# A one-core vision layer on TensorE: the first images' grey computed on DVE, the key projection as three fp32r products, and the experts' output added to the stored residual by DMA transfers

## The reference

```python
gray  = einsum('bchw,c->bhw', x, (0.2989, 0.587, 0.114))
edge  = (|conv3x3(gray, scharr_x)| + |conv3x3(gray, scharr_y)|) / 2      # h
n     = layernorm(h);  ns = n shifted by one token
k, v, r = (n*tm_i + ns*(1-tm_i)) @ W_i.T        for i in k, v, r
y     = wkv(w, u, k, v)                          # running max, two scans over the tokens
h     = h + (sigmoid(r) * y) @ Wo.T
n2    = layernorm(h);  e = argmax(n2 @ Wg.T)    # one of 8 experts per token
h     = h + gelu((layernorm(n2)*s_e + b_e) @ W1_e + b1_e) @ W2_e + b2_e  # result
```

## Time and profile before

| what | value |
|---|---|
| median of the runs | 1195.4 us |
| the profiled execution | 1192.23 us |
| its span, first to last instruction | 1190.7 us |
| PE busy, share | 1109.3 us, 93% |
| DVE busy, share | 1003.7 us, 84% |
| ACT busy, share | 858.2 us, 72% |
| mean granted TensorE clock | 0.981 of full |

### The profile page before, as it was taken

One profiled execution on the slowest core, in us unless ns is written; L12 is line 12 of the kernel. 1 busy time (PEld: TensorE's weight loads), 2 busy tenths in 40 slices (PEclk: granted clock), 3 DMA queues, 4 the chain that ended last, 5 costly groups with the idle time before them and its releaser, 6 DMA issues.

```text
span 1190.7 us, 16854 instructions
## 1 busy us (share of the span) xinstructions
PE 1109.3 (93%) x5571; PEld 696.7 (59%) x5571; DVE 1003.7 (84%) x1828; ACT 858.2 (72%) x1380; POOL 177.3 (15%) x242
## 2 busy tenths in 40 slices
PE   1277799999999999999999999999999999999997
PEld 0033366666666666656666666656666666666666
DVE  1257999999998999999999999999998999999971
ACT  2046788777777787777777877777778877777652
POOL 5211101111111110111110101111101111110000
PEclk9967899999999999999999999999999999999999
DMA  7997756776676766776767667766766677662001
GB/s 187 207 169 121 133 127 128 149 154 140 136 151 150 139 134 134 158 143 135 147 146 146 132 129 159 153 132 136 158 145 123 137 149 153 141 102 47 18 18 36
DMA packets 164837, 157.79 MB, mean 133 GB/s; under 512 B 12528, under 2 KB 164678, under 8 KB 164678
## 3 DMA queue, kind: packets, MB, share of 16 engines
q1 hardware_dynamic: 129990, 123.84, 42.7%
q0 software_dynamic: 34816, 33.56, 22.3%
HBM read 105.96 MB, written 68.17 MB: 146 GB/s over the span
## 4 chain that ended last, share of the span: by engine, by line
PE 90%; DMA 3%; DVE 3%; ACT 2%; SPq 1%; issue 0%; POOL 0%; POOLq 0%; DVEq 0%
PE bank L1008 28%; PE bank L1144 18%; PE bank L1074 15%; PE bank L1002 10%; PE bank L1050 9%; PE bank L1096 4%; DMA rows_in<-gray_dram 2%; PE bank L1122 2%; PE bank L1145 1%; DMA gray_dram<-planes 1%; PE bank L1087 1%; PE bank L1131 1%; PE bank L1063 1%; SPq L329 1%; DMA scharr_dj<-in_L_tok_scharr_dram 0%
## 5 line engine op out<-in xcount | busy, mean ns | idle before, releaser
L1144 PE MATMUL bank<-w_sb,hidden 128*128 128x256 f32 x1024 | 238.8, 380 | 0.8 <-ACT hidden L860 0.8
L1144 PEld LDWEIGHTS bank<-w_sb,hidden 128*128 128x128 f32 x1024 | 184.6, 190 | 29.2 <-ACT hidden L860 1.5
L1002 PE MATMUL bank<-rows_in,conv_w 102*32 102x512 f32 x1024 | 129.9, 628 | 31.5 <-DMA rows_in<-gray_dram 31.5
L1008 PE MATMUL bank<-mixed_k,w_k_t 128*128 128x512 f32 x256 | 127.5, 622 | 4.1 <-DVE mixed_k L557 4.1
L1008 PE MATMUL bank<-mixed_r,w_r_t 128*128 128x512 f32 x256 | 118.6, 607 | 4.8 <-DVE mixed_r L557 4.8
L1074 PE MATMUL bank<-normed_hi,w_hi 128*128 128x512 f32 x256 | 122.2, 477 | 0.0
L1008 PE MATMUL bank<-mixed_v,w_v_t 128*128 128x512 f32 x256 | 120.1, 592 | 0.0
L568 DVE TENSOR_TENSOR_SCAN max_state<-neg_exp_w,bank 128x256 f32<-128x256 f32 x128 | 80.7, 672 | 45.3 <-PE bank L1008 45.3
L1050 PE MATMUL bank<-w_o_t,rwkv 128*128 128x256 f32 x512 | 117.5, 382 | 0.0
L403 POOL TENSOR_TENSOR pool_turn<-pool_turn 128x1 f32<-128x1 f32 x32 | 7.9, 246 | 663.1 <-ACT planes L784 663.1
L1050 PEld LDWEIGHTS bank<-w_o_t,rwkv 128*128 128x128 f32 x512 | 94.9, 190 | 12.0 <-issue 0.5
(11 more groups left out here) (132 smaller groups left out, 2230.5 us busy)
## 6 DMA issues: line engine op xcount, KB each, us to landing
rows_in<-gray_dram SPq DMA_DIRECT2D x192, 256.0 KB
planes<-in_x_dram SPq DMA_DIRECT2D x128, 256.0 KB, 5.0
gray_dram<-planes POOLq DMA_DIRECT2D x128, 256.0 KB, 6.1
gray_dram<-in_x_dram SPq DMA_DIRECT2D x64, 256.0 KB, 6.5
out_dram<-resid SPq DMA_DIRECT2D x64, 256.0 KB, 2.2
rows_in<-gray_dram SPq DMA_DIRECT2D x128, 24.0 KB
gray_dram<-rows_in SPq DMA_DIRECT2D x1, 1032.0 KB
hidden<-in_L_ffn_W_dram SPq DMA_DIRECT2D x2, 256.0 KB, 10.3
```

The lines of the kernel that those rows point to most:

```text
L1002: ins = pe.matmul(bank[BANK_EDGE[n]][ROW_TILE * q:ROW_TILE * (q + 1), :], conv_w[0:TAPS, c, :], rows, start=True, stop=True)
L1008: ins = pe.matmul(ps[:, :], w_t[i][:, kt, ct * P:(ct + 1) * P], mixed[i][:, 2 * kt:2 * kt + 2, :].rearrange("p i t -> p (i t)"), start=(kt ...
L1144: pe.matmul(ps, hidden[:, m, i, rows], w2_sb[:, m, :], start=(m == 0), stop=False)
```

## The change

Five things are changed together.

1. The grey of pairs 0 and 1 is computed on DVE from planes loaded by SP and ACT (`first_gray_of`), and stored to `gray_dram` in one go. From pair 2 on (`has_later`) the way of the grey is as before.
2. `rows_in` has two buffers. SP's step loads the planes and the blue earlier than before, behind other waits.
3. The key projection takes three fp32r products per half, of `w_hi`, `w_lo`, `part_hi`, `part_lo`. ACT makes the high part of the mixed input (`high_part`), DVE the low part (`low_part`).
4. DVE's `result` is gone. SP stores the residual already in the PROJ stage. ACT copies the experts' output from PSUM to `y_out` (`copy_y`), and POOL starts two transfers that add it to the stored output (`add_y`).
5. The orders of all engines, the PSUM banks and the places of the setup are new. `route_logits` and `copy_logits` moved from the end of a step to the start of the next.

```diff
+FIRST = 2
+SPLIT = (0,)
+    def has_later(self, stage):
+        return self.has(stage) and (not isinstance(self.j, int) or UNROLL * self.j + self.u - stage >= FIRST)
-        rows_in = sb("rows_in", [P, TILES, 2, D])
+        rows_in = [sb(f"rows_in{i}", [P, TILES, 2, D]) for i in range(2)]
+        y_out = [sb(f"y_out{i}", [P, NB, D]) for i in range(2)]
...
@@ SP step
+                if at.has_later(LOAD):
+                    b = at.buf(LOAD)
+                    wait(sp, s_green, at.count(LOAD, 16 * HALF, 16 * HALF, back=2 + FIRST))
...
+                    load_plane(0, at.j, at.u, b)
+                    wait(sp, s_edge_ps, at.count(LOAD, 4, 4, back=3))
+                    load_plane(1, at.j, at.u, b)
+                    wait(sp, rows_loaded[b], at.dma_count(LOAD, X_DMAS, back=2))
+                    load_blue(at.j, at.u, b)
+                if at.has_later(GRAY):
...
+                    for i in range(2):
+                        load_rows(sp, b, i)
+                if at.has(PROJ):
+                    b = at.buf(PROJ)
                     for half in range(HALF):
+                        wait(sp, s_resid, at.count(PROJ, 2, half + 1))
+                        sp.dma_start(out_rows(at.j, at.u - PROJ, half), resid[b][:, 2 * half:2 * half + 2, :]
+                                     ).then_inc(stored[b], 16)
@@ POOL
+            def add_y(at):
+                if not at.has(FFN):
+                    return
+                b = at.buf(FFN)
+                wait(pool, s_out_turn, at.count(FFN, 1, 0))
+                wait(pool, stored[b], at.dma_count(FFN, HALF))
+                wait(pool, s_y_out, at.count(FFN, 2, 2))
+                pool.tensor_tensor(out_turn[:, :], out_turn[:, :], out_turn[:, :], ALU.add).then_inc(s_out_turn, 1)
+                for half in range(HALF):
+                    pool.dma_start(out_rows(at.j, at.u - FFN, half), y_out[b][:, 2 * half:2 * half + 2, :],
+                                   accum_op=ALU.add).then_inc(added[b], 16)
@@ DVE
+            def first_gray_of(i):
+                for half in range(HALF):
+                    rows = slice(2 * half, 2 * half + 2)
+                    total = first_gray[i][:, rows, 1:D + 1]
+                    dve.wait_ge(first_in[i][half], 48)
+                    dve.scalar_tensor_tensor(out=total, in0=planes[i][:, rows, 0, :],
+                                             scalar=GRAY_WEIGHTS[0] / GRAY_WEIGHTS[2], in1=first_blue[i][:, rows, :],
+                                             op0=ALU.mult, op1=ALU.add).then_inc(s_first_mix, 1)
...
+            def low_part(i, stage, low_done, at):
...
+                dve.tensor_tensor(part_lo[i][:, :, :], mixed[i][:, :, :], part_hi[i][:, :, :].bitcast(F32),
+                                  ALU.subtract).then_inc(low_done, 1)
-            def result(half, at):
...
@@ PE
+                products = [(w_t[i], mixed[i])]
+                if i in SPLIT:
+                    products = [(w_hi[i], part_hi[i]), (w_lo[i], part_hi[i]), (w_hi[i], part_lo[i])]
...
@@ ACT
+            def high_part(i, stage, high_done, at):
...
+                act.activation(part_hi[i][:, :, :], mixed[i][:, :, :], ACT.Copy).then_inc(high_done, 1)
+            def copy_y(half, at):
...
+                act.activation(y_out[b][:, 2 * half:2 * half + 2, :], pair_view(bank[BANK_Y[half]]), ACT.Copy
+                               ).then_inc(s_y_out, 1)
             def step(at):
-                scaled(0, at)
-                scaled(1, at)
                 absolute(0, at)
+                copy_logits(at)
                 reciprocal(at)
                 absolute(1, at)
                 absolute(2, at)
+                scaled(0, at)
+                scaled(1, at)
                 absolute(3, at)
```

More of the change, by code:

```diff
@@ L311, in step @@
             def step(at):
-                if at.has(LOAD) and not at.first():
-                    wait(sp, s_green, at.count(LOAD, 16 * HALF, 16 * HALF, back=2))
-                    load_planes(at.j, at.u, at.buf(LOAD))
-                if at.has(LOAD) or at.has(GRAY):
-                    wait(sp, s_edge_ps, at.count(LOAD, 4, 4, back=2))
-                if at.first():
-                    sp.wait_ge(s_borders, 32)
-                if at.has(LOAD):
-                    load_blue(at.j, at.u, at.buf(LOAD))
@@ L660, in best_logit @@
             def best_logit(at):
-                if not at.has(PROJ):
+                if not at.has(FFN):
                     return
-                wait(dve, s_logits, at.count(PROJ, 1, 1))
+                wait(dve, s_logits, at.count(FFN, 1, 1))
                 dve.tensor_reduce(best[:, :], logits, AXIS_X, ALU.max).then_inc(s_best, 1)
@@ new lines, in _, with decay_rate @@
+            act.wait_ge(s_cleared, CLEARED_B2)
+            for r, src in rows:
+                act.dma_start(params_raw[r:r + src.shape[0], :], src).then_inc(s_params_in, 16)
+            act.dma_start(w_raw[2], Wr.rearrange("(a p) c -> p a c", p=P)).then_inc(s_w_in, 16)
+            act.wait_ge(first_stored[1], 16 * HALF)
+            load_rows(act, 1, 1)
+            def decay_rate(at):
+                if not at.is_step(EDGE):
+                    return
+                act.wait_ge(s_dve_setup, SETUP_PARAMS)
+                act.activation(exp_w[:, :], params[:, ROW_W:ROW_W + CH], ACT.Exp).then_inc(s_act_setup, 1)
@@ L1016, in project_k @@
                 if ct == 0:
-                    wait(pe, s_mix_k, at.count(WKV, 1, 1))
-                else:
-                    wait(pe, s_normed2_lo, at.count(WKV, 2, 1, back=2))
+                    wait(pe, s_low_k, at.count(WKV, 1, 1))
+                elif ct == 1:
+                    wait(pe, s_abs, at.count(WKV, 4, 1, back=-1))
                 project(0, ct, bank[BANK_K[ct]], s_k_ps)
@@ L1045, in output_projection @@
                 if half == 0:
-                    wait(pe, s_abs, at.count(PROJ, 4, 4, back=-2))
                     wait(pe, s_rwkv, at.count(PROJ, 1, 1))
+                elif half == 1:
+                    wait(pe, s_abs, at.count(PROJ, 4, 2, back=-2))
                 for i in range(2):
@@ L1057, in transpose_route @@
                     return
-                wait(pe, s_abs, at.count(FFN, 4, 2, back=-3))
                 wait(pe, s_route, at.count(FFN, 1, 1))
@@ L1102, in transpose_normed2 @@
                 if ct == 0:
-                    wait(pe, s_hidden, at.count(PROJ, 4, 1, back=1))
                     wait(pe, s_normed2, at.count(PROJ, 1, 1))
@@ L1137, in second_layer @@
                     wait(pe, s_hidden, at.count(FFN, 4, 4))
-                else:
-                    wait(pe, s_gate, at.count(FFN, 2, 1, back=-2))
                 for i in range(2):
```

532 lines of the change are left out of this document (310 added, 222 removed).

## The result

The changed kernel takes 1179.98 us (median of 4 runs, 1178.11 to 1180.79), the kernel before 1194.87 beside it. The ratio is 0.9873, with a 95% interval of 0.9854 to 0.9892: 1.3% faster. The profiled execution has a span of 1177.8 us, against 1190.7.

The account below looks back on a forecast made before the run. PE was taken to set the steady step, with the grey's loop closing it after the change. Filling -18, steady part +2 and emptying +6 sum to -10, on 1195.4 giving 1185 us, range 1166 to 1222.

Parts of the forecast that it names:

- The likeliest case: Steady steps: the grey closes the step at 33.4 to 34.4 us, giving 1172 to 1200 us; chance 0.50.
- The loop: Way of the grey, once per step: red's turn 8.0, red 7.5, green 6.7, rows 11.5; with jitter, 33.9 us.
- The steady term: The 27 steady steps: 33.9 us each, 0.1 more than before, together +2 us.
- Red's open length: Red's accumulating transfer in the loop: between 6.9 and 9.75 us, taken as 7.5.
- The rival of 1242 us: Steady steps: red stays at 9.75 us, the grey bounds a step of 36.0 us, +47 us; chance 0.27.
- The adding transfer: `add_y` on POOL: issued 1 to 2 us into the step, its traffic ending at about 8 to 9.
- PE's work: Key products on PE: two halves save 0.68 us a step, so PE needs 33.1 us.
- The filling: Start of the program up to pair 4's convolution, which comes at 153: -18 us (10 to 24).
- The emptying: End of the program: last copy and accumulating transfer +4, `low_part` wait in step 34 +2.8 less 0.7; together +6 us.
- The clock rival: Steady steps: waits at step starts drop PE to 1.2 GHz, loop 37.1 us, +77, 1272 us; chance 0.05.

Follow-up runs that it names:

- e1: The changed kernel with the two scalings of the planes back at the head of ACT's step from step 5 on; 1164.8 us (ratio 0.9763).
- e2: The changed kernel with the key projection again as f32 products, without high_part and low_part; 1186.38 us (ratio 0.9937).
- e11: The changed kernel with red and green planes from pair 2 on loading 16 of 256 columns, scaling set to 0.5; 1164.73 us (ratio 0.9764).
- e5: The kernel before with the two scalings behind the third absolute value of the edges from step 5 on; 1193.95 us (ratio 1.0005).
- e4: The changed kernel with the adding transfer moving only 16 of the 256 columns of each row; 1179.92 us (ratio 0.9883).
- e6: The kernel before with only the key projection changed to three fp32r products (high_part on ACT, low_part on DVE); 1180.09 us (ratio 0.9894).
- e3: The changed kernel with scalings early from step 5 on and the key projection again in f32; 1179.6 us (ratio 0.9876).
- e7: The changed kernel with all pairs' grey by accumulating DMA, the first two too, and the padded buffer zeroed whole; 1207.94 us (ratio 1.0129).
- e9: As e7, against the changed kernel, but with the scalings at the head of every step of ACT; 1182.44 us (ratio 0.9916).
- e10: The changed kernel with scalings at the head of every step and the later weights one step later in SP's queue; 1160.23 us (ratio 0.9725).

## Why the prediction was right

Forecast 1185, range 1166 to 1222; measured 1180.0. The likeliest case, the grey closing the step at about its old length, is what happened. The sum was -10 and became -12.9 in the profiled spans (14.9 in the medians), but two terms were off by 7 and 8 us, in opposite directions. That they nearly cancel is luck.

- **The loop.** Right in mechanism, shown by e1 and e2: the idle time stands before `convolve(0)`, its releaser is "DMA rows_in", and the split's gain mostly vanishes into it. I had 8.0 + 7.5 + 6.7 + 11.5 and a little for jitter, 33.9; the means are 7.56 + 6.98 + 6.84 + 12.22 = 33.60. Turn and red were too long by 0.4 and 0.5, and the rows 0.7 too short, so that the four added up to 33.7 by luck too. On the rows, the read of the earlier trace rows is of a quiet moment, while now the DMA share at the same point is 1.1. I had the next planes move in the first 8 to 9 us of a step; they are issued 6.4 us ahead of `convolve(0)` (624.75, 631.17), while the rows are still on their way, and e11 shows what that costs. The window:

```profile
629.00:630.00 1.00, 1.00 (x7) 0.74 (x5) 1.00 (x3) 1.00 (x2) 0.00 (x0) 1.00 1.09 221
```

- **The steady term, +2, measured -5.9.** The mis-sized term: 33.9 against 33.60, 0.3 us a step times 27 is 8 us. Of the 0.3, 0.2 are what I added for jitter. Every guess of a tenth in a loop that runs 27 times weighs 3 us.
- **Red's open length.** I set 7.5 between 6.9 and 9.75, arguing that it starts when the traffic is nearly over. e5 shows the later start as cause: moved alone, it drops from 9.71 to 7.13. That it is the traffic of the planes fits their landings, but no run removed them beside an early red. The rival of 1242 us needed 9.75 in the late place, and there was none.
- **The adding transfer.** I took its traffic as ended by 8 to 9 us; it lands at 9.0, and by e4 its last 1.5 us beside the red cost nothing. In e1, where the red starts 1.5 us behind it, the red takes 8.9 in the mean. The Trainium skill, DMA: Bandwidth & Descriptors, section Queues, rings and completion order, says that each DMA engine takes the descriptors of a queue in order. In e1 the trace agrees: the adding transfer lands at 9.3 us, the two halves of the red at 11.6 and 13.4. That this order is what makes e1's red longer is not shown, since before, with no adding transfer, the red took 9.71 us at that place.
- **PE's work.** 0.68 predicted for the split, 0.64 (before to e6) and 0.65 (e3 to e1) measured. PE needs 32.9 a step, not 33.1. The other 0.3 are in e3 too (33.53 against 33.82, both without waits), so they come with the rest of the change, in which the products stand in another order. I had not priced that, and haven't taken it apart.
- **The filling, -18, measured -11.3.** The first convolution came at 33.3, not 28, pair 1's at 48.4, not 43, pair 2's at 86.65, not 84: its scaling ended at 58.9, not 57, its red's turn came at 59.66, and the 27 us from there were as predicted. Pairs 2 to 4 were to take 34.5 us each, and took 34.69 and 37.94. In the second PE waits for `low_part`, and its clock falls for a while. PE's timeline:

```profile
128.85 0.57 PE L1167 MATMUL bank<-part_k_hi,w_k_hi 128*128 128x512 f32 x1 [2.59 <-DVE part_k_lo L651]
```

The windows around it (the clock is the third number from the end):

```profile
126.00:131.00 5.00, 2.41 (x10) 1.70 (x7) 5.00 (x6) 5.00 (x8) 0.00 (x0) 0.81 0.00 0
131.00:136.00 5.00, 5.00 (x21) 4.10 (x20) 3.80 (x8) 0.97 (x2) 2.59 (x3) 0.84 0.53 54
```

I had found that wait for step 34 and not asked for it here, the other step where DVE's list runs behind. Without the split (e2, e3) this step takes 36.3 us. But e1 keeps the split and takes 35.8, without that wait and at a mean clock of 0.92, so how much of the 37.94 is the split's stays open. And I missed what e7 showed: late scalings cost the filling too, 16.5 us when all pairs go the old way. With them the early grey is worth 34 us (e7 to the changed kernel), and much of it pays for the late scalings; with early ones it is 19.6 (e9 to e10, which also differ in the place of the later weights).
- **The emptying, +6, measured +4.4.** PE waits 2.54 us at step 34's key products, as worked out (2.8), and the last transfer ends 7.85 us after the turn. Before, the last addition started 3.5 us ahead of the end: +4.35, where I had 4. The other 2.1 us (2.8 less 0.7) did not appear: from pair 31's `convolve(0)` to that last turn or addition it is 103.4 us in both kernels, so some 2 us came back elsewhere, and I haven't taken that apart. The two lines:

```profile
1102.60 0.50 PE L1167 MATMUL bank<-part_k_hi,w_k_hi 128*128 128x512 f32 x1 [2.54 <-DVE part_k_lo L651]
...
1169.95 0.18 POOL L469 TENSOR_TENSOR out_turn<-out_turn 128x1 f32<-128x1 f32 x1 [13.64 <-ACT y_out L1031]
```

The size also depends on the execution. The emptying of e5 runs the same operations as before's, yet takes 2.9 us longer, at a granted clock of 0.97 instead of 1.00 (before, then e5):

```profile
1083.82:1190.70 106.88, 97.14 (x492) 67.24 (x484) 69.40 (x133) 55.56 (x90) 0.00 (x0) 1.00 0.07 23
1084.63:1194.40 109.77, 99.99 (x492) 69.08 (x484) 69.46 (x133) 55.58 (x90) 0.00 (x0) 0.97 0.07 22
```

- **The clock rival.** It did not come for good: over the 907 us the granted clock is 1.00 in the mean. But it showed once. Behind the longest wait at a step's start, 1.89 us, PE fell to its 1.2 GHz level, and the convolution took 4.38 us instead of 2.78. PE's timeline, and the windows behind it:

```profile
732.27 4.38 PE L1157 MATMUL bank<-rows_in,conv_w 102*32 102x512 f32 x24 [1.89 <-DMA rows_in<-gray_dram]
...
733.00:734.00 1.00, 1.00 (x12) 0.28 (x8) 1.00 (x2) 0.60 (x1) 1.00 (x2) 0.65 0.59 156
734.00:736.00 2.00, 2.00 (x16) 0.49 (x12) 0.76 (x2) 0.00 (x1) 1.84 (x2) 0.50 1.04 255
736.00:737.00 1.00, 1.00 (x20) 0.59 (x16) 0.00 (x0) 0.00 (x0) 0.00 (x0) 0.64 0.93 171
```

In e4 the same happened behind a wait of 1.93 us at 329.3, and not behind those of 1.84 and 1.79. So this kernel was closer to the clock rival than its mean clock says.

So the steady part gains 23.8 us with early scalings (27 x 0.88, e1), of which the split gives 17.3 (e6), and the late scalings take 17.8 of it back (27 x 0.66). The early grey's gain is partly a repair of what late scalings do to the filling. The additions by DMA were not needed for the step and cost 4.35 us at the end. Undoing the late scalings alone is worth 15.2 us by the medians and 13 by the ratios, about as much as the whole change (14.9).

## What to carry to other kernels

Write out every loop that must close once per step, with its slack, and compare its length with the bounding engine's work; an edit that makes that engine cheaper is worth only as much as the loops have slack. When an operation moves, recompute the transfer behind it at its new time: traffic that it met before may be gone. And an order that only delays something in steady state may tie steps together in the filling, where there is no steady overlap to hide it.

## What the runs showed of the hardware that was not expected

- The same accumulating transfers of 2 x 256 KB by POOL take 7.0 to 7.1 us from turn to turn in one place of the step and 8.4 to 9.7 in another, in kernels that otherwise agree: the start decides, and a delay of 5.0 us cost only 2.4 at the end of the red.
- With the adding transfer cut to a sixteenth of its bytes (q0 from 48.25 to 32.52 MB), the steady step did not shrink: 33.76 against 33.60 us.
- Many small waits of PE, 16.1 us in 27 steps, left the granted clock at full but for one place: behind a wait of 1.89 us it was at its half level for part of 733 to 737. In e4 a wait of 1.93 us did the same, and waits of 1.84 and 1.79 us did not. In the filling a wait of 2.59 us was followed by the half level for part of 129 to 133; in the emptying one of 2.54 us was not in the changed kernel, and was in e1.
- Two emptyings with the same operations, before and e5, took 106.9 and 109.8 us, at granted clocks of 1.00 and 0.97.
